# A group search by pairs of tiles on four engines, and attentions and a gated product with a semaphore for each weight

## The reference

```python
# L1_ffn
h = silu(x @ wg.T) * (x @ wu.T);  out = h @ wd.T        # weights int32, times 1/127
# L3_ffn, the search of the groups
sim = (qg_n * q_n).sum(-1).mean(-1)                     # cosine of each head with the vector g, mean over 16 heads
sim = (sim - sim.min()) / (sim.max() - sim.min())
pos = sim > 0.9                                         # two masks of keys from this
# attentions (L0, L2, L3, L3_ffn)
softmax(q @ k.T * scale) @ v @ wo + bo                  # L3 keeps 32 scores of a row
```

## Time and profile before

| | us |
|---|---|
| median of 3 runs | 2816.24 |
| lowest, highest | 2799.23, 2816.45 |
| profiled execution, its time | 2813.1 |
| its span | 2811.3 |
| mean granted clock of TensorE | 0.767 |
| PE, DVE, ACT, POOL busy | 2037.6, 1657.5, 1097.2, 1003.1 |

### The profile page before, as it was taken

The page is one execution under the profiler, slowest core; times in us unless marked ns, Lnnn a source line. Parts: engine busy times, 40 slices in busy tenths (PEclk is TensorE's granted clock), DMA queues, the critical chain, the costliest instruction groups (busy, mean ns, idle before and its releaser), DMA issues. The chain is left out here.

```text
span 2811.3 us, 41872 instructions
## 1 busy us (share of the span) xinstructions
PE 2037.6 (72%) x13025; PEld 1632.3 (58%) x13025; DVE 1657.5 (59%) x5348; ACT 1097.2 (39%) x3087; POOL 1003.1 (36%) x1053
## 2 busy tenths in 40 slices
PE   6983788499159869834989907777777777763995
PEld 4653788399138756534888805555555555542663
DVE  5763000388962258640101138999999999935773
ACT  3551222355021125411322206666666666610443
POOL 3312222400000056224222245666666666504440
PEclk9995899755569979957999956676667666556997
DMA  2112554410000011124354230000000000000112
GB/s 84 63 62 74 210 181 171 127 28 1 0 34 1 12 34 62 63 101 166 112 175 139 94 97 8 8 9 8 1 8 8 1 1 1 1 6 23 36 46 72
DMA packets 99753, 163.61 MB, mean 58 GB/s; under 512 B 19774, under 2 KB 78038, under 8 KB 91606
## 3 DMA queue, kind: packets, MB, share of 16 engines
q1 hardware_dynamic: 77112, 79.62, 8.9%
q0 software_dynamic: 22464, 81.83, 8.3%
HBM read 191.23 MB, written 39.35 MB: 82 GB/s over the span
## 5 line engine op out<-in xcount | busy, mean ns | idle before, releaser
L546 DVE MATCH_REPLACE8 l3a_left<-l3a_top,l3a_left 128x256 f32<-128x256 f32 x768 | 310.0, 413 | 0.0
L539 DVE MAX8 l3a_top<-l3a_left 128x8 f32<-128x256 f32 x768 | 287.1, 417 | 0.0
L357 POOL TENSOR_TENSOR l3a_prob<-l3a_expd,l3a_rest 128x512 f32<-128x512 f32 x128 | 162.5, 1269 | 230.6 <-ACT l3a_rest L437 230.5
L264 PE MATMUL l3a_psT<-all_ident,l3a_prob 128*128 128x128 f32 x512 | 124.0, 388 | 162.2 <-POOL l3a_prob L357 162.2
L282 PE MATMUL l3a_psO<-l3a_probT,l3a_vp 128*128 128x128 f32 x1024 | 214.5, 375 | 28.8 <-ACT l3a_probT L453 28.8
L282 PEld LDWEIGHTS l3a_psO<-l3a_probT,l3a_vp 128*128 128x128 f32 x1024 | 184.1, 269 | 81.2 <-ACT l3a_probT L453 47.9
L264 PEld LDWEIGHTS l3a_psT<-all_ident,l3a_prob 128*128 128x128 f32 x512 | 83.8, 197 | 185.6 <-POOL l3a_prob L357 185.2
L344 POOL TENSOR_TENSOR l3a_kept<-l3a_raw_sc,l3a_mone 128x512 f32<-128x512 f32 x128 | 163.0, 1274 | 57.7 <-ACT l3a_raw_sc L421 57.1
L1602 ACT ACTIVATE l2f_ffn_hT<-l2f_ffn_psH,l2f_ffn_wt 128x128 f32<-128x128 f32 x312 | 89.0, 368 | 229.7 <-PE l2f_ffn_psH L1557 190.4
L1557 PE MATMUL l2f_ffn_psH<-l2f_ffn_xsT,l2f_ffn_wt 128*128 128x128 f32 x1248 | 154.0, 284 | 29.6 <-DMA l2f_ffn_wt<-in_L_table,l2f_ffn_idx 28.2
L437 ACT ACTIVATE l3a_rest<-l3a_left,l3a_nmax 128x256 f32<-128x256 f32 x256 | 116.1, 502 | 150.6 <-DVE l3a_left L546 149.8
(11 more groups left out here) (492 smaller groups left out, 4749.5 us busy)
## 6 DMA issues: line engine op xcount, KB each, us to landing
l2f_ffn_xs<-slots_x SPq DMA_DIRECT2D x39, 128.0 KB
slots_y<-l2f_ffn_y SPq DMA_DIRECT2D x39, 128.0 KB
slots_x<-l2f_route_zero SPq DMA_DIRECT2D x19, 256.0 KB, 3.0
o_at<-l0a_oraw SPq DMA_DIRECT2D x16, 256.0 KB, 2.0
l0a_osum<-o_at SPq DMA_DIRECT2D x32, 128.0 KB
o_at<-l2a_oraw SPq DMA_DIRECT2D x16, 256.0 KB, 2.0
l2a_osum<-o_at SPq DMA_DIRECT2D x32, 128.0 KB
o_at<-l3f_oraw SPq DMA_DIRECT2D x16, 256.0 KB, 2.0
```

Source lines behind the costliest of these rows:

```text
L264: mm = nc.tensor.transpose(psT[u % 2][:, kc, e, :], prob[:, u % 4, e, kc * P:kc * P + P], ident[:])
L357: nc.gpsimd.tensor_tensor(prob[:, u % 4, :, :], expd[:, u % 2, :, :], rest[:, u % 2, :, :], ALU.subtract).then_inc(picked, 1)
L539: ins = nc.vector.max(top[:, e, eight], rows[:, e, :] if r else scores[:, e, :])
L546: ins = nc.vector.match_replace(out=rows[:, e, :], in_to_replace=top[:, e, eight], in_values=rows[:, e, :] if r else scores[:, e, :], imm_ ...
```

## The change

- Search: ACT normalises two tiles at once (scale and offset per row), copies the transposes of the pair, squares PSUM straight into `sq` and takes roots by pair; DVE multiplies PSUM with the scaled g and sums heads by pair, the cosines of a pair one pair later. PE turns pair b+1 before it multiplies pair b. PSUM and SBUF tiles are doubled. The mean over heads becomes a sum (the next step scales it away). The second group of row statistics stands behind the first operations on g, the vector to compare with; g is loaded ahead of wq. The tail has a slightly other order.
- Gated product: PE's first transposes no longer wait for weights; u is scaled on ACT, between the two roots; g is scaled on DVE ahead of the second group of statistics, d behind it; PE waits for g and u before the first product, for d before the first `down`.
- Picked attention: `k_in` (wk, bk, bq, even), `q_in`, `w_in` (wv, wo, bv, bo); loads reordered, the first mask before wv; DVE scales the bias and reads the mask ahead of its second statistics and of the memset; ACT's second root moves behind the first queries.
- Paired attention: `q_in` (wq, even, biases of columns, cos, sin), `k_in`, `v_in`, `w_in` (the rest). PE transposes with no wait for loads; the waits for `w_in` and `m_in` come behind the second transposes. POOL adds `bo` in `add_bias`, for the first two sequences behind `k_parted(0)`.

```diff
 # picked_attention, sync / tensor / scalar / vector
+            sp.dma_start(even[:], evens).then_inc(k_in, 16)
+            sp.dma_start(W["wq"][:], w["wq"].rearrange("(c p) n -> p c n", p=P)).then_inc(q_in, 16)
+            load_mask(0)
...
-            pe.wait_ge(w_in, 16 * n_w)
+            pe.wait_ge(k_in, 64)
             keys(0)
             x_turned(0)
+            pe.wait_ge(q_in, 16)
             queries(0)
             scores(0)
+            pe.wait_ge(w_in, 64)
...
-            stats.roots(act)
+            stats.root(act, 0)
...
+            stats.root(act, 1)
             copy_scores(0)
 # paired_attention, tensor
+            x_turned(0)
+            for what, there, n in (("q", q_in, n_q), ("k", k_in, 1), ("v", v_in, 1)):
+                pe.wait_ge(there, 16 * n)
+                projected(0, what)
+            x_turned(1)
             pe.wait_ge(w_in, 16 * n_w)
             if groups is not None:
                 pe.wait_ge(m_in, 16 * 17)
-            x_turned(0)
...
 # paired_attention, gpsimd
-            if "bo" in Br:
-                pool.wait_ge(w_in, 16 * n_w)
             normalise(0)
             normalise(1)
-            pool.wait_ge(w_in, 16 * n_w)
             nc.gpsimd.memset(nm[:].rearrange("p b q c n -> p (b q c n)"), 0.0).then_inc(nm_zero, 1)
+            pool.wait_ge(q_in, 16 * n_q)
...
             k_parted(0)
+            pool.wait_ge(w_in, 16 * n_w)
+            add_bias(0)
+            add_bias(1)
 # gated_ffn, tensor / scalar
+                if not again:
+                    pe.wait_ge(w_set, 1)
+                    pe.wait_ge(up_set, 1)
...
-            pe.wait_ge(w_set, 3)
+            pe.wait_ge(x_norm, 1)
             up(0, 0, False)
             up(1, 1, True)
+            pe.wait_ge(w_set, 2)
             down(0, 0)
...
+            act.wait_ge(w_in[1], 16)
+            nc.scalar.activation(W["u"][:].rearrange("p c n -> p (c n)"), raw["u"][:].rearrange("p c n -> p (c n)"), ACT.Copy, scale=QSCALE)\
+                .then_inc(up_set, 1)
 # find_groups, tensor
+            turn(0)
             pe.wait_ge(w_in, 48)
...
+            for b in range(B):
+                if b + 1 < B:
+                    turn(b + 1)
+                queries(b)
 # find_groups, scalar
+            stats.root(act, 0)
+            normalise(0)
+            normalise(1)
             act.wait_ge(g_in, 1)
             nc.scalar.activation(gs[:], gn[:], ACT.Sqrt).then_inc(g_out, 1)
...
+            stats.root(act, 1)
+            read_t(0)
+            for b in range(B):
+                if b + 2 < B:
+                    normalise(b + 2)
+                if b + 1 < B:
+                    read_t(b + 1)
+                square(b)
+                if b:
+                    lengths(b - 1)
+            lengths(B - 1)
 # find_groups, vector
+            def sums(b):
+                dve.wait_ge(squared, b + 1)
+                nc.vector.tensor_tensor(by[:, b % 2, :, :].rearrange("p (t m) d -> p t (m d)", t=QT), psQ[b % 2][:],
+                                        gq[:].rearrange("p h d -> p (h d)").unsqueeze(1).to_broadcast([P, QT, D]), ALU.mult)\
+                    .then_inc(multiplied, 1)
+                nc.vector.tensor_reduce(n2[:, b, :], sq[:, b % 2, :, :], AX.X, ALU.add).then_inc(n2_set, 1)
+                dve.wait_ge(multiplied, b + 1)
+                nc.vector.tensor_reduce(dot[:, b, :], by[:, b % 2, :, :], AX.X, ALU.add).then_inc(dot_set, 1)
...
+            for b in range(B):
+                sums(b)
+                if b:
+                    cosines(b - 1)
+            cosines(B - 1)
```

More of the change, by code:

```diff
@@ L2266, in then, with offsets, cosines @@
                 dve.wait_ge(step, n[0])
+            def offsets(g):
+                a, z = stats.tiles(g)
+                dve.wait_ge(stats.done, g + 1)
+                nc.vector.scalar_tensor_tensor(out=offset[:, a:z], in0=mean[:, a:z], scalar=-1.0, in1=rstd[:, a:z], op0=ALU.mult, op1=ALU.mult)\
+                    .then_inc(off_set, 1)
+            def sums(b):
[6 more added lines that the diff above has]
+                nc.vector.tensor_reduce(dot[:, b, :], by[:, b % 2, :, :], AX.X, ALU.add).then_inc(dot_set, 1)
+            def cosines(b):
+                dve.wait_ge(rooted, b + 1)
+                dve.wait_ge(dot_set, b + 1)
+                then(nc.vector.reciprocal(over[:, b, :], root[:, b, :]))
+                then(nc.vector.tensor_tensor(dot[:, b, :], dot[:, b, :], over[:, b, :], ALU.mult))
+                ins = nc.vector.tensor_reduce(sim[:, b * QT:b * QT + QT], dot[:, b, :].rearrange("p (t h) -> p t h", t=QT), AX.X, ALU.add)
+                if b == B - 1:
+                    then(ins)
             stats.moments(dve, 0)
-            stats.moments(dve, 1)
-            dve.wait_ge(stats.done, 2)
+            offsets(0)
             dve.wait_ge(w_in, 48)
```

225 lines of the change are left out of this document (114 added, 111 removed).

## The result

The changed kernel took 2742.14 us (median of 4 runs), the kernel before in the same rounds 2816.34: a ratio of 0.975, 95% interval 0.970 to 0.980. The forecast was 2756, the range 2734 to 2782: direction and time came out as said, with somewhat more saved than the 58.0 us of the sum. The profiled run spans 2737.1 us where that of before spans 2811.3: 74.2 us less. The rest of this text asks where they are, because 58.0, 65.8 and 74.2 are not the same number.

What follows compares the result with a forecast made beforehand. Stages run one after the other, so what ends last in each bounds it; in the search that was DVE's work after PE's tiles. Terms summed to 58.0 us off 2813.1, giving 2755.1, written as 2756; range 2734 to 2782.

Steps and rivals of the forecast that it cites:

- Search, 41.7: Search: work by tile pairs over three engines, period 2.7 us at full clock, cosines done at 2505.0; 41.7 us saved.
- Clock: Search: cold, PE has no idling, so the clock rises; warm, it stays; wholly cold saves 31.7 instead of 41.7 us.
- Rival 1: Search: clock stays at 1.2 GHz or swings; 48.0 us saved in all, 2766 us; chance 0.18.
- Gated product, 5.1: Gated product's start: first product 6.0 us earlier through u scaled on ACT, minus 0.9 for starting cold; 5.1 us (3.5 to 6.3).
- Picked attention, 6.9: Picked attention's start: PE waits only for wk, biases and `even`, queries at 1681.6 against 1688.52; 6.9 us (3 to 9).
- l2a, 2.3: Paired attention l2a: ACT's first copy waits for the second root, queries start at 987.75 instead of 990.05; 2.3 us.
- l3f, 1.1: Paired attention l3f: POOL's empty 7.53 us stays, PE starts at 2567.3 and not 2568.49; 1.1 us.
- l0a, 0.9: Paired attention l0a: if POOL first stands 7.5 us as in l3f, normalising begins 0.9 us earlier (0 to 2.8).
- Bias additions and last weights, nothing: Paired attentions' bias additions (2 x 1.27 us on POOL) and gated product's last weight scaling are hidden; no time gained or lost.
- Starts eaten: All early starts, 16.3 us together, are absorbed by other waits or the clock; 41.7 us saved, 2772 us; chance 0.08.
- Gated product cold: Gated product begins after idling and stays at half clock; wholly cold, the kernel ends at 2892 us; chance 0.02.
- Pairs in sequence: Search bound by hand-overs, each pair taking 9.9 us in sequence; loses 9, gains 16, 2806 us; chance 0.02.

Runs made afterwards that it cites:

- t1: Changed kernel with the starts of search, picked attention and paired attentions reordered again, nothing computed otherwise: 0.9741 of the kernel before.
- e3: Changed kernel, but PE in the search turns the next pair only after the current one is copied, multiplied and read: 2781.9 us, one run; search 68.2 us.
- e4: Kernel before, with four 128-column products of no use per tile in the old search, ahead of PE's wait for DVE's copy: 2801.9 us, one run; search 74.3.
- e2: Changed kernel with the old search, so the new starts alone: 0.9945 of the kernel before, 15.5 us saved.
- c1: Changed kernel unaltered, measured again in later rounds: 0.9766 of the kernel before, 65.8 us saved.
- w1: Changed kernel, where PE fills idle time at the stages' starts with transposes of the identity that nobody reads: 0.9742 of the kernel before, 2739.5 us.
- t3: Changed kernel with starts reordered again, cosines two pairs at a time, g and u in two parts, and idle time filled with transposes: 0.9706, 2730.6 us.

## Why the prediction was right, step by step

Shown is first what the step said, then what the runs measured.

- **Search, 41.7.** Stage length 44.9 less in five profiles. The mechanism is the one told; two sizes were off. The period is 2.49 us, not 2.7, because a DVE operation that reads nothing of the one ahead starts 0.08 us before that one's listed end (0.60 from 2465.27 to 2465.87 with 0.68 of duration): some 0.2 us a pair, 1.4 over seven. And the first pair was through earlier: first product 10.1 us after the start instead of 10.9. The clock came up 4.8 us after it, 5 was the forecast; over five profiles it is 4.5 to 6.1, so the step had the middle of a scatter. The price of the first copy queued behind the second root (up to 2.5 us at DVE's first product, t1) wasn't called a loss, since the count gave no gain here.
- **Clock.** "Cold it leaves PE no idling, so it should rise; warm, it should stay": so it was, in every profile of the search as changed (43.0 to 44.0). Rival 1 fell. That the same stage's clock does swing once the buffers don't cover is shown (e3), and that the old loop sat at 0.50 because of 0.52 us of idling per tile too (e4).
- **Gated product, 5.1.** Stage 5.5 us shorter, first silu 5.5 us earlier on average (19.3 to 20.4 us after the stage's start in three old profiles, 14.1 to 14.7 in four new). Two errors cancelled. The landing of u was put at 6.3 us after the start; in the profile above it took 7.5 us from issue instead of 5.9 and came at 7.8, in the three others at 6.6 to 6.9, so the first product came 5.3 us earlier on average and not 6.0. And the 0.9 for a lost head start of the clock was not lost: the clock rose 3.1, 5.5 and 5.1 us after the first product with the old start, 3.0, 5.2, 4.0 and 4.8 with the new. That the old kernel's four transposes 1.9 us ahead of its product had given it a head start was an inference from one trace, and such a difference lies within the scatter. That the term came out near is luck.
- **Picked attention, 6.9.** First MAX8 8.7 us earlier in six of six profiles. Keys and queries came as counted (first query product 9.4 us after the start, 9.5 forecast). The step left out that queries and scores, close behind the keys, would run at full clock: 1.97 instead of 3.78 us. It also said that the memset has 4 us of cover; DVE lost 1.96 us to the second root and MAX8 waited for the memset by about 0.8. t1 took both away: 16.5 us instead of 18.8.
- **l2a, 2.3.** First query product 8.2 us after the stage's start instead of 10.5, first output tiles 2.3 us earlier.
- **l3f, 1.1.** 0.7 by the first output tiles: in the profile above the empty stretch on POOL, taken as fixed at 7.53 us, was 8.02, and PE's first transposes came 0.7 us earlier for it (13.0 us after the stage's start, 13.7 before). The stretch is 7.4 to 8.0 in seven profiles. The rest of the 2.8 by which the stage is shorter is not shown to be the change's.
- **l0a, 0.9.** Wrong: 2.6 by the first output tiles, close to the upper bound given (2.8). The row of l3f (7.53 us with nothing in it ahead of POOL's first operation) was carried over to l0a, where such an instruction stands in the order too. There POOL began 2.5 us after the stage's start. "POOL in l0a begins at once" was named as what would show the step wrong, and it did. Why l3f's stretch is there and l0a's isn't wasn't tried.
- **Bias additions and last weights, nothing.** No wait for them ends last in the starts shown.
- **Rivals 2 to 4.** Starts eaten: e2 has them all, 15.5 us alone (10 to 21) against 16.3 forecast. Gated product cold: granted clock 0.97. Pairs in sequence: made to order in e3, it costs 25 us (68.2 against 43.4), and even so stays under the old 88.3.

The sum by what was measured: 44.9 + 9.8 + 5.5 + 1.7 + 2.8 + 2.6 = 67.3 in place of 58.0, with c1 at 65.8. The 58.0 was low for the search (3.2), for the picked attention (1.8 by its first MAX8) and for l0a (1.7).

## What to carry to other kernels

Ask of a slow stage first whether its engines take turns: here one engine's long passes at the end, cut into pieces of one tile pair and spread over three engines, gave some two thirds of the search's gain, and a third could be had from the clock alone. Where PE idles a little in every step and the granted clock reads 0.50, a few products of no use are a one-line test (e4) of what the clock is worth, and idle time filled right ahead of a stage's first product is worth up to 1.9 us where little idling follows it: the clock held behind 1.54 us in w1's search and fell behind 1.71 and 0.78 in t3's l2a. Reorder starts by what ends the wait in the bracket. Read the worth from the first product or first output after the stage's start, and not from the stage's length, which scatters by several microseconds.
